# One stage for a finish and a projection, rope by pairs, and a re-ordered last stage in a float32 kernel on one Trainium2 core

## What is computed

```
1 x = x + ln(attn8(ln(x)) @ Wout.T)             16 heads of 8, scores clipped, causal
2 x = x + ln(latent(ln(x)))                     h = xx + attention(rms(xx)), xx = ln(x)
      q = rms(xx) @ Wq         (16 heads: 32 plain + 32 rope)
      ckv = rms(xx) @ Wkva     (16 latent + 32 rope, shared by the heads)
      rope: (x0, x1) -> (x0 cos - x1 sin, x0 sin + x1 cos) for each pair
      out = h + experts(rms(h))                 top 2 of 8, one shared
3 x = x + ln(attn8(ln(x)))                      16 heads of 8, causal
4 x = x + ln(gelu(ln(x) @ U1 @ V1 + b1) @ U2 @ V2 + b2)
```

## Time and profile before

| what | us |
|---|---|
| runs before, median of 3 | 2229.62 (2224.72 to 2230.24) |
| profiled execution, its own time | 2222.28 |
| its span, first to last instruction | 2220.6 |
| finish_heads8 and project_latent, from the end of attention a0 to the begin of attention am | 411 to 621.7 |
| finish_latent | 1273 to 1325.5 |
| finish_and_ffn | 2091.5 to 2220.6 |
| project_heads8, p0 and p1 | 41 to 107, 1544 to 1609 |
| busy: PE, DVE, ACT, POOL | 1750.1, 1351.4, 1110.9, 652.9 |

### The profile page before, as it was taken

The page is one execution under the profiler, slowest core; times in us unless marked ns, Lnnn a source line. Parts: engine busy times, 40 slices in busy tenths (PEclk is TensorE's granted clock), DMA queues, the critical chain, the costliest instruction groups (busy, mean ns, idle before and its releaser), DMA issues. The chain is left out here.

```text
span 2220.6 us, 42674 instructions
## 1 busy us (share of the span) xinstructions
PE 1750.1 (79%) x12448; PEld 730.9 (33%) x12448; DVE 1351.4 (61%) x2596; ACT 1110.9 (50%) x1754; POOL 652.9 (29%) x1169
## 2 busy tenths in 40 slices
PE   3378878657728999999999778997469989899576
PEld 3212222333303433343434264543223333233232
DVE  1568887545536665665666044555578878788162
ACT  0389999432203554554555523231317767677453
POOL 1445555335411322231222100112412222222252
PEclk9789999779957999999999987998859999999876
DMA  3542222413331322131311040000522222211311
GB/s 93 195 100 72 71 73 51 86 53 103 106 64 26 69 46 58 35 68 36 68 35 45 32 140 1 0 0 1 190 60 51 51 51 51 51 51 32 68 29 29
DMA packets 89058, 135.27 MB, mean 61 GB/s; under 512 B 23777, under 2 KB 52833, under 8 KB 88802
## 3 DMA queue, kind: packets, MB, share of 16 engines
q1 hardware_dynamic: 88898, 133.11, 23.9%
HBM read 78.56 MB, written 54.39 MB: 60 GB/s over the span
## 5 line engine op out<-in xcount | busy, mean ns | idle before, releaser
L897 ACT ACTIVATE q_buf<-ps 128x1024 f32<-128x1024 f32 (+1 forms) x1152 | 863.5, 822 | 557.9 <-PE ps L784 556.6
L981 DVE TENSOR_REDUCE o_sb<-ps 128x1 f32<-128x512 f32 (+3 forms) x864 | 719.4, 866 | 297.0 <-PE ps L813 193.2
L945 POOL TENSOR_SCALAR_AFFINE_SELECT q_buf<-q_buf 128x256 f32<-128x256 f32 x768 | 364.1, 498 | 855.2 <-ACT q_buf L897 700.7
L833 PE MATMUL ps<-q_buf,v_buf 128*16 128x512 f32 (+7 forms) x4608 | 464.6, 499 | 56.9 <-POOL q_buf L945 54.4
L784 PE MATMUL ps<-q_buf,k_buf 49*128 49x512 f32 (+3 forms) x1536 | 325.4, 525 | 8.1 <-issue 8.1
L784 PE MATMUL ps<-q_buf 48*128 48x512 bf16 (+7 forms) x1536 | 260.8, 335 | 73.2 <-DMA v_buf<-v_d 32.2
L1033 DVE TENSOR_SCALAR q_buf<-q_buf 128x1024 f32<-128x1024 f32 x288 | 215.6, 754 | 68.2 <-ACT q_buf L897 62.9
L784 PEld LDWEIGHTS ps<-q_buf 48*128 48x128 bf16 (+1 forms) x1536 | 76.5, 94 | 323.3 <-ACT q_buf L897 222.8
L784 PEld LDWEIGHTS ps<-q_buf,k_buf 49*128 49x128 f32 x1536 | 133.3, 191 | 137.9 <-ACT q_buf L897 66.6
L833 PEld LDWEIGHTS ps<-q_buf,v_buf 128*16 128x16 f32 (+1 forms) x4608 | 97.4, 100 | 231.3 <-issue 116.1
L806 PE MATMUL ps<-k_buf,q_buf 48*128 48x512 bf16 (+3 forms) x768 | 119.9, 345 | 62.0 <-DVE o_sb L981 29.9
(11 more groups left out here) (167 smaller groups left out, 1676.5 us busy)
## 6 DMA issues: line engine op xcount, KB each, us to landing
q_buf<-q_d SPq DMA_DIRECT2D x384, 32.0 KB
qm_d<-q_buf SPq DMA_DIRECT2D x48, 256.0 KB
q_buf<-qm_d SPq DMA_DIRECT2D x32, 384.0 KB
v_d<-q_buf SPq DMA_DIRECT2D x16, 512.0 KB
v_buf<-v_d SPq DMA_DIRECT2D x32, 256.0 KB
o_d<-pr_buf SPq DMA_DIRECT2D x128, 64.0 KB, 2.0
q_buf<-o_d SPq DMA_DIRECT2D x16, 512.0 KB, 7.3
o_d<-pr_buf SPq DMA_DIRECT2D x16, 512.0 KB, 2.7
```

Of the source, the lines that this page charges most:

```text
L833: mm = nc.tensor.matmul(ps[VW * j:VW * j + V_ROWS_OUT, o_bank + half % O_BUFS, lo * P:(lo + nq) * P], v, units(i, r, j)[:, 0, off * P:(off ...
L897: nc.scalar.activation(units(i, g, WIDE * e, WIDE), ps[:, bank:bank + WIDE, :], ACT.Exp, scale=scale).then_inc(s_e, 1)
L945: nc.gpsimd.affine_select(out=blk, in_=blk, compare_op=ALU.is_ge, fill=0.0, base=0, pattern=[[0, 2], [1, P]], channel_multiplier=-1)\
L981: nc.vector.tensor_reduce(to, sc, AX_X, ALU.max).then_inc(s_mr, 1)
```

## The change

Five things are changed.

- finish_heads8 and project_latent become one stage, finish_and_project_latent, of steps c = -4 to 7. In step c chunk c is in the latent projection, c+1 in the second norm, c+2 in the first norm, c+3 in the output projection, c+4 in the output turns. All is written out, without a hardware loop.
- Rope rows are laid out by pair members: one matmul gives the first members of eight heads, one the second members. Each of the two results is multiplied by cos and by sin (four products), and POOL joins them by a difference and a sum. The latent rows share one slot of two banks. So there are four slots of two matmuls per chunk.
- There are no squares: the root mean square of xx follows from the variance of x, var/(var + eps), so xr = (x - mean) * (var (1 + eps) + eps^2)^-1/2 comes from one pass of statistics, applied by ACT. xx itself is no longer stored. POOL computes its scales at the end of the stage (rstd_xx, shift_xx), and finish_latent's ACT builds xx from x.
- In project_heads8 ACT applies the norm, not DVE; POOL's first two inverses stand ahead of its memset.
- In finish_and_ffn the output turns are five chunks ahead instead of four, the result has two PSUM banks, the second rank takes the bank of the turned x (its own is given up), and the orders on all engines are changed. DVE now applies norm2 ahead of its wait for the result; norm3 is applied on ACT one step later.

```diff
@@ project_heads8: the vector, GpSimd and scalar queues
-        def apply(c):
-            dve.wait_ge(s_T, c - 1 + BASE) if c > 1 else None
-        norm.stats(dve, 0, tiles(x_res, 0))
-        norm.stats(dve, 1, tiles(x_res, 1))
-        apply(0)
-        norm.stats(dve, 2, tiles(x_res, 2))
-        apply(1)
-        norm.stats(dve, 3, tiles(x_res, 3))
+        for c in range(4):
+            norm.stats(dve, c, tiles(x_res, c))
         for c in range(CHUNKS):
             u = c % 2
-            if c + 2 < CHUNKS:
-                apply(c + 2)
...
         pool.wait_ge(s_begin, BASE)
+        for c in range(2):
+            norm.inverse(pool, c)
         nc.gpsimd.memset(v_pad, 0.0).then_inc(s_pad, 1)
-        for c in range(4):
+        for c in range(2, 4):
             norm.inverse(pool, c)
...
+            norm.apply_act(act, c, tiles(x_res, c), xn[:, c % 2, :, :])
+        apply(0)
+        apply(1)
         copy_turned(0)
         copy_turned(1)
         for c in range(CHUNKS):
+            if c + 2 < CHUNKS:
+                apply(c + 2)
@@ in place of finish_heads8 and project_latent (both removed)
+def finish_and_project_latent(wo):
...
+LOADS, ONS, HALF, PR = 3, 3, CT // 2, 3
+turn_bank, T2_bank, y_bank, T_bank, slot0 = 0, 1, 2, 3, 4
+STEPS = range(-4, CHUNKS)
+SLOTS, K_SLOT, LAT_SLOT = 4, 0, 2
...
+        for c in range(LOADS):
+            load(c)
+        for n in TABLES:
+            sp.dma_start(table[n], consts[n]).then_inc(s_tab, 16)
+        for c in range(LOADS, LOADS + 2):
+            load(c)
...
+            sp.wait_ge(s_rot, ROTS * c + 1 + BASE)
+            sp.dma_start(km_d[b, :, tok], values(c, 0)[0:MD, :]).then_inc(s_st[u], 16)
+            sp.wait_ge(s_vp, c + 1 + BASE)
+            sp.dma_start(vm_d[b, :, u * CT:(u + 1) * CT, :], v_pad[:, u, :, :]).then_inc(s_vst[u], 16)
+            if c + LOADS + 2 < CHUNKS:
+                load(c + LOADS + 2)
...
+        def turn_x(c):
+            pe.wait_ge(s_xr, c + 1 + BASE)
+            if c > 0:
+                pe.wait_ge(s_vp, c + BASE)
+            transpose_chunk(T_bank, xr[:, c % 2, :, :]).then_inc(s_T, 1)
...
+        def slot(c, i):
+            if i == K_SLOT:
+                pe.wait_ge(s_xT, c + 1 + BASE)
+                if c > 0:
+                    pe.wait_ge(s_lat, 2 * c + BASE)
+                rows, wa, wb = MD, w_sb["wkva"][:, :], w_sb["wkva_sw"][:, :]
+            elif i == LAT_SLOT:
+                pe.wait_ge(s_pr, ROTS * c + 1 + BASE)
+                rows = P
+                wa, wb = (wabs[:, half, :, :, :].rearrange("p a b c -> p (a b c)") for half in range(2))
+            else:
+                hp = i // 2
+                if c + hp > 0:
+                    pe.wait_ge(s_pr, ROTS * c + (3 if hp else 0) + BASE)
+                rows, wa, wb = P, w_sb["wq_rope"][:, hp, 0, :], w_sb["wq_rope"][:, hp, 1, :]
+            for bank, w in zip(slot_banks(i), (wa, wb)):
+                mm = nc.tensor.matmul(ps[0:rows, bank, :], w, xrT[:, c % 2, :], start=True, stop=True)
+            mm.then_inc(s_mm, 1)
...
+        for c in STEPS:
+            if there(c):
+                slot(c, 0)
+                latent_values(c)
+            if there(c + 3):
+                turn_normalised(c + 3)
+            if there(c):
+                slot(c, 1)
+            if there(c + 4):
+                turn_outputs(c + 4, 0)
+            if there(c):
+                slot(c, 2)
+            if there(c + 3):
+                out_projection(c + 3)
+            if there(c + 1):
+                turn_x(c + 1)
+            if there(c):
+                slot(c, 3)
+            if there(c + 4):
+                turn_outputs(c + 4, 1)
...
+        for c in STEPS:
+            if there(c + 2):
+                if c + 2 > 1:
+                    act.wait_ge(s_x1, c + 1 + BASE)
+                norm1.apply_act(act, c + 2, ps[:, y_bank, :].rearrange("p (t c) -> p t c", c=C),
+                                z1[:, (c + 2) % 2, :, :])
+            if there(c + 3):
+                copy_normalised(c + 3)
+            if there(c + 1):
+                apply_rms(c + 1)
+            if there(c):
+                copy_latent(c, 0)
+                copy_latent(c, 1)
+            if there(c + 1):
+                copy_turned(c + 1)
...
+        def join(c, m):
+            pool.wait_ge(s_pr, ROTS * c + m + 1 + BASE)
+            if c > 1 and m == 0:
+                pool.wait_ge(s_st[c % 2], 16 * VALS * (c // 2) + BASE)
+            rows, r = (MD, P)[m > 0], (ROTS * c + m) % PR
+            nc.gpsimd.tensor_tensor(values(c, m)[0:rows, :], t_a[0:rows, r, :], t_b[0:rows, r, :],
...
+        for c in STEPS:
+            if there(c + 2):
+                norm1.inverse(pool, c + 2)
+            if there(c + 1):
+                inverse_rms(c + 1)
+            if there(c):
+                for m in range(3):
+                    join(c, m)
+            if there(c + 2):
+                add(c + 2)
+            if there(c):
+                for m in range(3, ROTS):
+                    join(c, m)
+        nc.gpsimd.tensor_scalar(rstd_xx[:, :], mv_xx[:, :, 1], EPS, None, ALU.add).then_inc(s_xx, 1)
+        nc.gpsimd.tensor_scalar(shift_xx[:, :], mv_xx[:, :, 0], -1.0, None, ALU.mult).then_inc(s_xx, 1)
+        for c in range(CHUNKS):
+            at = slice(c * CT, (c + 1) * CT)
+            pool.wait_ge(s_xx, 2 + c + BASE)
+            nc.gpsimd.tensor_tensor(rstd_xx[:, at], rstd_xx[:, at], minus_half[:, :], ALU.pow)\
+                .then_inc(s_xx, 1)
+        pool.wait_ge(s_xx, 2 + CHUNKS + BASE)
+        nc.gpsimd.tensor_tensor(shift_xx[:, :], shift_xx[:, :], rstd_xx[:, :], ALU.mult).then_inc(s_xx, 1)
...
+        def products_q(c, hp):
+            i = 1 + 2 * hp
+            dve.wait_ge(s_mm, SLOTS * c + i + 1 + BASE)
+            a, b = slot_banks(i)
+            free_products(c, i)
+            product(t_a, c, i, P, a, "cos_q")
+            product(t_b, c, i, P, b, "sin_q").then_inc(s_pr, 1)
+            free_products(c, i + 1)
+            product(t_a, c, i + 1, P, a, "sin_q")
+            product(t_b, c, i + 1, P, b, "cos_q").then_inc(s_pr, 1)
...
+        for c in STEPS:
+            if there(c + 2):
+                dve.wait_ge(s_y, c + 3 + BASE)
+                norm1.collect(c + 2, ps[:, y_bank, :].rearrange("p (t c) -> p t c", c=C))
+            if there(c + 1):
+                dve.wait_ge(s_x1, c + 2 + BASE)
+                for t in range(CT):
+                    i = nc.vector.bn_stats(bn2[:, (c + 1) % 2, t, :], x_res[:, (c + 1) * CT + t, :])
+                i.then_inc(s_bn2, 1)
+            if there(c + 2):
+                norm1.aggregate(dve, c + 2)
+            if there(c + 1):
+                dve.wait_ge(s_bn2, c + 2 + BASE)
+                for t in range(CT):
+                    i = nc.vector.bn_aggr(mv_xx[:, (c + 1) * CT + t, :], bn2[:, (c + 1) % 2, t, :])
+                i.then_inc(s_mv2, 1)
+            if there(c):
+                if c == 0:
+                    dve.wait_ge(s_tab, 16 * len(TABLES) + BASE)
+                products_k(c)
+            if there(c + 4):
+                normalise(c + 4, 0)
+            if there(c):
+                products_q(c, 0)
+                copy_values(c)
+            if there(c + 4):
+                normalise(c + 4, 1)
+            if there(c):
+                products_q(c, 1)
@@ finish_latent: the scalar queue; its Fori loop is written out
+            act.wait_ge(s_x2, 2 * b + u + 1 + BASE)
+            for t in range(CT):
+                at = (2 * b + u) * CT + t
+                i = nc.scalar.activation(xx[:, u, t, :], x_res[:, at, :], ACT.Identity,
+                                         scale=rstd_xx[:, at:at + 1], bias=shift_xx[:, at:at + 1])
+            i.then_inc(s_xx, 1)
...
-                tiles_of(xx_res, b, u), ALU.add).then_inc(s_x2, 1)
+                xx[:, u, :, :], ALU.add).then_inc(s_x2, 1)
@@ finish_and_ffn
-turn_bank, x_bank, q_bank, y_bank, h_bank0 = 0, 1, 2, 3, 4
+turn_bank, x_bank, y_bank0, h_bank0 = 0, 1, 2, 4
-STEPS = range(-4, CHUNKS + 2)
+STEPS = range(-5, CHUNKS + 3)
...
     def turn_x(c):
         pe.wait_ge(norm2.s_out, c + 1 + BASE)
-        if c > 0:
-            pe.wait_ge(s_pT, c + BASE)
+        if c > 1:
+            pe.wait_ge(s_qT, c - 1 + BASE)
...
     def result(c):
-        if c > 0:
-            pe.wait_ge(norm3.s_out, c + BASE)
+        if c > 1:
+            pe.wait_ge(norm3.s_out, c - 1 + BASE)
...
     for c in STEPS:
+        if there(c):
+            hidden(c)
         if there(c + 1):
             turn_x(c + 1)
-        if there(c):
-            hidden(c)
-        if there(c + 4):
-            turn_outputs(c + 4, 0)
+        if there(c + 5):
+            turn_outputs(c + 5, 0)
         if there(c + 1):
             first_rank(c + 1)
+        if there(c + 5):
+            turn_outputs(c + 5, 1)
         if there(c - 1):
             result(c - 1)
-        if there(c + 4):
-            turn_outputs(c + 4, 1)
         if there(c):
```

(58 more changed lines are left out.)

532 lines of the change are left out of this document (234 added, 298 removed).

## The result

The changed kernel takes 2309.18 us (median of 4 runs, 2305.58 to 2311.95), the kernel before 2229.93: a ratio of 1.036, 95% interval 1.033 to 1.038. It is 79 us **slower**; the forecast was 2160 us, a gain of 70.

The account below looks back on a forecast made before the run. It took engines waiting on each other, none filled, as the bound. Terms -49.3 (merged stage), -19 (last stage), -1.0 (projections), -0.4 (weight transfer) sum to -69.7 us: profiled 2152.6, median 2160 us; own range 2145 to 2180, wider 2138 to 2192.

Parts of the forecast that it names:

- The step that failed: Merged stage: 1.7 MB of stores plus 0.5 MB of loads per chunk take under 9 us, hidden in 14.2.
- The rival of late loads: Merged stage: a load inside the stores lands 12 instead of 8 us after issue; +10 us, 2170; chance 0.15.
- signs named in the prediction: Merged stage: the forecast is wrong if PE waits for the loads, or if the granted clock is near 0.5.
- The slower rival: Merged stage: low clock makes steps 23 us, eight cost 71; 2272 us with the last stage low; chance 0.03.
- The steady step: Merged stage: 14.2 us from the end of DVE's last product of one chunk to that of the next.
- The stage's start: Merged stage: four steps ahead of chunk 0 take 31 us, step 0 takes 18; step 1 begins at 471.3.
- POOL's tail: End of merged stage: after a last join, POOL prepares the scales of xx in 10.4 us, longer than the last store.
- the term: Whole merged stage: the attention behind it begins at 572.4, a gain of 49.3 us; bounds -64 to -33.
- The clock with many transposes: Merged stage: by the skill's rule transposes don't count for PE's clock, making 2272 us likely; the forecast held the trace against it.
- Finish of the latent attention: There ACT's four added applies (1.6 us) per chunk fit in its waits: cost 0, at most 13 us.
- The projections: Both stages projecting the 8-wide heads: only an earlier first store helps; -1.0 us together, between 0 and -2, above +1.
- The last stage: finish_and_ffn: steps of 8.3, then 6.7 to 6.9 us, two at the low clock; -19 us, bounds -29 to +22.

Follow-up runs that it names:

- e3: The kernel before, with only its four rope stores per chunk reshaped to 16 rows of two items instead of 32 rows of one: 2346.7 us.
- e1: The changed kernel, with each of its six qm_d stores per chunk issued as two stores of one item, 64 rows each: 2154.59 us.
- e8: e1 with q8_d laid out with the part outermost, so a q store in project_heads8 has one outer dimension of 128 rows: 2135.4 us.

## Why the prediction was wrong

- **The step that failed** is the sentence on the transfers: 1.7 MB of stores "at the 97 GB/s of the stage, where the share is 0.35, this is under 9 us of transfer in 14.2: hidden". The working comes out only if the 97 GB/s at a share of 0.35 are scaled up to all 16 engines: 277 GB/s, and 2.2 MB of stores and loads in 8 us. So it took for granted that any transfer can use all 16, and it put in an average over stores of two shapes. The new shape uses 2 of them: the rate is 51 GB/s, one chunk costs 31.3 us instead of 14.2, and the merged stage took 299.1 us where 150 were forecast. I wrote that the transfers per chunk stay; the bytes did, the shape did not. The rival of late loads named the right queue, but sized it at 10 us in all; the forecast missed by 149. Two of the signs named in the prediction did come, as consequences: PE waited for the loads behind the stores (48.1 us in three waits), and the granted clock was 0.50 in the windows above, 0.66 over the stage.
- **The slower rival** named the low clock. The clock did fall, behind PE's waits, but it was not the cause: e3 is as slow without the new stage, and e1, with it and with the same matmuls, has 0.98 from the end of chunk 0's products to the end of the last.
- **The steady step** was right to 2%: 14.2 forecast, 13.98 in e1, and DVE's wait stands where I said, ahead of the second half's reciprocal, on PE (4.25 us, forecast about 3). From the last product of chunk 0 to that of chunk 7 it is 87.8 us in e1 (476.4 to 564.2), 87.7 in the sum. DVE's queue of e1 at the end of a step:

```profile
501.10 0.36 DVE L1373 RECIPROCAL q_buf<-ps 128x32 f32<-128x32 f32 x1 [4.25 <-PE ps L1180]
501.49 0.42 DVE L1377 TENSOR_TENSOR q_buf<-ps,q_buf 128x256 f32<-128x256 f32 x1
501.83 2.47 DVE L1383 TENSOR_TENSOR q_buf<-ps,k_buf 128x512 f32<-128x512 f32 x4
504.22 0.88 DVE L260 BATCH_NORM_STATS2 q_buf<-ps 128x6 f32<-128x128 f32 x4
```

- **The stage's start** took 45.3 us to the end of chunk 0's products, 48.9 forecast. **POOL's tail** took 9.7, 10.4 forecast, and it did set the end. With spread stores the merged stage is 53.9 us shorter than before; the term was 49.3.
- **The clock with many transposes**: in e1 the two windows above have 1.00, with 24 transposes in every step, so the low clock that the prediction took from the rule of the Trainium skill (TensorE: Matmul & The Clock Gate, Part 4) did not come. That alone does not refute the rule: the 33 other matmul records of a step fill 10.0 of its 13.98 us. The finish of the latent attention in the kernel before weighs more: from 1285 to 1320 us the granted clock is 1.00, with transposes (L1436, L1445) busy for 21.9 us and the other matmuls for 13.6. No run here tests the rule apart.
- **Finish of the latent attention**: cost 0 forecast; with experts 265.4 before, 265.1 after. Right.
- **The projections**: -1.0 forecast, +4.1 and +1.8 measured. Also here the stores bound, which I had seen, but not why (e8).
- **The last stage**: -19 forecast, -27.4 measured. Chunk 0's hidden layer begins 24.4 us behind the first turn (24.7 forecast), and the last three steps are 6.6 us each (6.7 to 6.9 forecast). I had put two late steps at the low clock, 10 us; the trace has one stretch of it, 2264.6 to 2268.3, worth 1.6 us.
- **The sum without the failed step** is e1: 2154.59 us against 2160; in the traces -67.6 us where -69.7 were forecast. That is closer than the terms are, by luck in part: the merged stage gave 4.6 us more than forecast and the last stage 8.4, the projections 6.9 less, and all other stages together came out 7.7 longer.

## What to carry over

When an edit changes the shape of a transfer, cost the transfer anew, from a window in which only transfers of that shape run, and never from a stage's average rate. In this case a DMA share of 0.13 that did not move was the sign that two engines did all the work; there it helped to give the destination's outermost dimension 128 or 64 rows, by splitting the transfer (e1) or by laying out the tensor so that its rows merge (e8). Issues on SP that took 5 us instead of 0.6 came from a full queue, and what filled it was the thing to look at.
